# A graph attention layer: the mean row for nodes without edges in two float16 parts, and later waits in the first unit of a batch

## What is computed

```python
h = jnp.einsum('bnf,hfo->bhno', x, W)
s1 = jnp.einsum('bhno,ho->bhn', h, a1)
s2 = jnp.einsum('bhno,ho->bhn', h, a2)
e = leaky_relu(s1[..., :, None] + s2[..., None, :], negative_slope=0.2)
attn = softmax(where(adj > 0, e, -9e15), axis=-1)
h_prime = jnp.einsum('bhnm,bhmo->bhno', attn, h)
out = layernorm(x + h_prime.transpose(0, 2, 1, 3).reshape(B, N, H * Fo), axis=-1)
```

## Time and profile before

| what | value |
|---|---|
| time, median of 3 runs | 2936.99 us (2936.55 to 2944.32) |
| profiled execution, its time | 2935.6 us |
| its span, first to last instruction | 2933.7 us |
| PE busy | 2676.7 us (91%) |
| DVE busy | 2580.6 us (88%) |
| ACT busy | 2366.0 us (81%) |
| POOL busy | 823.3 us (28%) |

### The profile page before, as it was taken

One profiled execution on the slowest core, in us unless ns is written; L12 is line 12 of the kernel. 1 busy time (PEld: TensorE's weight loads), 2 busy tenths in 40 slices (PEclk: granted clock), 3 DMA queues, 4 the chain that ended last, 5 costly groups with the idle time before them and its releaser, 6 DMA issues.

```text
span 2933.7 us, 125924 instructions
## 1 busy us (share of the span) xinstructions
PE 2676.7 (91%) x52546; PEld 2318.7 (79%) x52546; DVE 2580.6 (88%) x3825; ACT 2366.0 (81%) x3950; POOL 823.3 (28%) x1011
## 2 busy tenths in 40 slices
PE   6999989989899898999989989899998999989996
PEld 3698867988579894898948988499884988859886
DVE  6899979998799997999889998899978999889896
ACT  4599964999559994699937998399983999839995
POOL 4522124221342214322152221521216222162221
PEclk9999999999999999999999999999999999999998
DMA  6567643676526754277533775347744477345763
GB/s 173 118 131 172 143 130 73 143 165 140 140 61 162 168 139 118 67 167 172 134 102 80 171 162 129 101 105 170 163 108 115 104 168 171 100 112 123 161 159 99
DMA packets 281205, 390.20 MB, mean 133 GB/s; under 512 B 161856, under 2 KB 161856, under 8 KB 280672
## 3 DMA queue, kind: packets, MB, share of 16 engines
q1 hardware_dynamic: 253536, 315.24, 41.6%
q0 software_dynamic: 27136, 67.12, 13.8%
HBM read 313.52 MB, written 34.14 MB: 119 GB/s over the span
## 4 chain that ended last, share of the span: by engine, by line
PE 31%; DVE 25%; ACT 22%; issue 16%; POOL 2%; DMA 2%; DVEq 1%; ACTq 0%; SPq 0%; POOLq 0%
ACT m_pos L602 20%; PE ps L525 11%; PE ps L556 6%; PE ps L557 6%; DVE m_neg L834 5%; PE ps L496 5%; DVE m_pos L827 3%; DVE m_pos L813 2%; DVE y L698 2%; DVE prod L800 2%; DMA y<-in_x 2%; ACT adj_cut L568 1%; DVE prod_d L803 1%; DVE total L665 1%; PE ps L432 1%
## 5 line engine op out<-in xcount | busy, mean ns | idle before, releaser
L602 ACT ACTIVATE m_pos<-ps,s_steep 128x512 fp8e4<-128x512 f32 x3496 | 2153.4, 1210 | 376.0 <-PE ps L446 281.9
L525 PE MATMUL ps<-b_both,m_pos 128*128 128x130 f16 x16384 | 1026.5, 222 | 113.1 <-DVE total L665 83.7
L525 PEld LDWEIGHTS ps<-b_both,m_pos 128*128 128x128 fp8e5 x16384 | 970.1, 99 | 127.5 <-issue 127.0
L557 PE MATMUL ps<-d_lo,m_neg 128*128 128x65 f16 x16384 | 1035.8, 194 | 24.1 <-issue 23.8
L556 PEld LDWEIGHTS ps<-d_hi,m_neg 128*128 128x128 fp8e5 x16384 | 1017.3, 98 | 37.4 <-issue 37.2
L556 PE MATMUL ps<-d_hi,m_neg 128*128 128x65 f16 x16384 | 1036.0, 193 | 4.0 <-issue 3.7
L557 PEld LDWEIGHTS ps<-d_lo,m_neg 128*128 128x128 fp8e5 x16384 | 1008.3, 98 | 19.4 <-issue 5.7
L827 DVE TENSOR_TENSOR m_pos<-m_pos,maskT 128x1024 uint32<-128x1024 uint32 x512 | 616.7, 1231 | 135.3 <-ACT m_pos L602 104.6
L834 DVE TENSOR_TENSOR m_neg<-m_pos,maskT 128x2048 uint32<-128x2048 uint32 x256 | 583.8, 2280 | 0.3
L496 PE MATMUL ps<-W_sb,xT 128*128 128x512 f32 x1024 | 459.4, 610 | 62.7 <-DVE prod_d L803 60.4
L568 ACT ACTIVATE adj_cut<-adj_in 128x1024 fp8e4<-128x1024 int32 x264 | 397.7, 1577 | 125.9 <-DMA adj_in<-in_adj 125.8
(11 more groups left out here) (95 smaller groups left out, 1606.7 us busy)
## 6 DMA issues: line engine op xcount, KB each, us to landing
adj_in<-in_adj SPq DMA_DIRECT2D x266, 512.0 KB, 4.9
s_bc<-s_rows SPq DMA_DIRECT2D x258, 256.0 KB, 3.8
x_in<-in_x SPq DMA_DIRECT2D x134, 256.0 KB, 4.7
x_sum<-in_x POOLq DMA_DIRECT2D x128, 256.0 KB, 5.8
y<-in_x POOLq DMA_DIRECT2D x32, 1024.0 KB, 9.8
out<-y SPq DMA_DIRECT2D x32, 1024.0 KB, 6.9
maskT<-adj_cut SPq DMA_TRANSPOSE x264, 4.0
m_neg<-in_x SPq DMA_DIRECT2D x10, 256.0 KB, 3.2
```

The source lines that it names most:

```text
L525: mm = pe.matmul(acc, mask, b_both[:, j, h, :, :], start=(j == 0 and it % 2 == 0), stop=(j == JC - 1 and it % 2 == 1))
L557: mm = pe.matmul(acc, mask, d_lo[:, j, h, :], start=False, stop=(j == JC - 1))
L602: ins = nc.scalar.activation(chunk(m_pos[h % 2], j, 0, BLK), ps[:, BANK_S1 + h % 2, :], ACT.Relu, bias=s2_steep[:, j, h:h + 1], scale=STEE ...
```

## The change

The mean row is cut into two float16 parts in place of three bfloat16 ones. `no_edge` multiplies the mean by the scale in partitions 0 to 63 (`mean_f`), casts it (`mean_part`), writes the cast to partition 0 of `mean_next` and the rest (float32 minus cast) to partition 32 (`LOW`). No memset and no multiplication with ident's columns is left. The very small constant moves from the mean row to the other operand, `tiny_bf`, in place of ones, and the product takes 64 partitions in place of 128. `mean_f` and `mean_next` are filled once at the start.

In PE's unit 0, quad 0 now waits for the low part b of chunk 7, quad 1 for that of chunk 12, and tile 0's j = 13, 14 and 15 each for their own. The wait for `hi_d_made` is gone, and x tile 0 is turned where the other tiles are: behind `spread_s1`, between the positive and the negative sums. Semaphores and tiles named tiny are named mean (those hunks are left out here). In PE's wait for the bank of the mean, `tiny_step` 6b + 1 is now `mean_step` 2b + 1.

```diff
@@ -86,6 +86,7 @@
+    LOW = 32
@@ -168,14 +169,15 @@
-        kappa_tiny = sb("kappa_tiny", [P, 1], F32)
+        kappa_mean = sb("kappa_mean", [P, 1], F32)
-        tiny_f = sb("tiny_f", [P, H, O1], F32)
-        tiny_part = sb("tiny_part", [P, H, O1], BF16)
-        tiny_next = sb("tiny_next", [P, H, O1], BF16)
-        tiny = sb("tiny", [P, H, O1], BF16)
+
+        mean_f = sb("mean_f", [P, H, O1], F32)
+        mean_part = sb("mean_part", [P, H, O1], F16)
+        mean_next = sb("mean_next", [P, H, O1], F16)
+        mean = sb("mean", [P, H, O1], F16)
@@ -487,7 +489,7 @@
-                        pe.wait_ge(tiny_step, 6 * b + 1)
+                        pe.wait_ge(mean_step, 2 * b + 1)
@@ -503,29 +505,31 @@
                         if unit == 0:
-                            pe.wait_ge(hi_d_made, b * JC + JC - 1)
-                            turn_x(JC * (b + 1), x_in[0][:], x_loaded[0], b * (JC // 2), 0)
-                            pe.wait_ge(tiny_made, b + 1)
-
-                            pe.wait_ge(lo_made, at(lo_made, 2 * JC * (b + 1) - 2))
+                            pe.wait_ge(mean_made, b + 1)
+
+                            pe.wait_ge(lo_made, at(lo_made, 2 * JC * b + JC - 1))
+                            pe.sem_inc(waited[pe.engine], 1)
                         pe.wait_ge(pos_read, at(pos_read, u))
                             pe.sem_inc(waited[pe.engine], 1)
+                            if unit == 0 and qd:
+                                pe.wait_ge(lo_made, at(lo_made, 2 * JC * (b + 1) - 7))
+                                pe.sem_inc(waited[pe.engine], 1)
                             for it in range(IT):
                                 for j in range(qd * JQ, (qd + 1) * JQ):
-                                    if unit == 0 and it == 0 and j == JC - 1:
-                                        pe.wait_ge(lo_made, at(lo_made, 2 * JC * (b + 1) - 1))
+                                    if unit == 0 and it == 0 and j >= JC - 3:
+                                        pe.wait_ge(lo_made, at(lo_made, 2 * JC * b + 2 * j + 1))
                                         pe.sem_inc(waited[pe.engine], 1)
                                     if j == 0:
-                                        pe.matmul(acc[:, 0:O1], ones_bf[:], tiny[:, h, :], start=False, stop=False)
+                                        pe.matmul(acc[:, 0:O1], tiny_bf[0:2 * LOW, :], mean[0:2 * LOW, h, :], start=False, stop=False)
                         mm.then_inc(pos_summed, 1)
@@ -535,7 +539,7 @@
                             turn_s1(b + 1)
-                        if unit and unit in TILE_UNIT:
+                        if unit in TILE_UNIT:
                             t = TILE_UNIT.index(unit)
@@ -739,30 +743,21 @@
                 dve.wait_ge(bound_step, 3 * n + 2)
                 V.tensor_scalar(kappa[:], bound_inv[:], SPLIT_TOP, None, ALU.mult)
-                V.tensor_scalar(kappa_tiny[:], bound_inv[:], SPLIT_TOP * TINY / N, None, ALU.mult
+                V.tensor_scalar(kappa_mean[:], bound_inv[:], SPLIT_TOP / N, None, ALU.mult
                                 ).then_inc(bound_step, 1)
                 dve.wait_ge(bound_step, 3 * n + 3)
-            def no_edge_start(n):
+            def no_edge(n):
+                both = slice(0, 2 * LOW)
                 dve.wait_ge(h_mean_summed, n + 1)
-                V.tensor_scalar(tiny_f[:, :, 0:O], ps[:, BANK_MEAN, :].rearrange("p (h o) -> p h o", h=H),
-                                kappa_tiny[:, 0:1], None, ALU.mult)
-                V.memset(tiny_f[:, :, O:O1], TINY * SPLIT_TOP).then_inc(tiny_step, 1)
-                dve.wait_ge(tiny_step, 6 * n + 1)
-
-            def no_edge_part(n, part):
-                V.tensor_copy(tiny_part[:], tiny_f[:]).then_inc(tiny_step, 1)
-                dve.wait_ge(tiny_step, 6 * n + 2 + 2 * part)
-                if part == 0:
-                    V.tensor_scalar(tiny_next[:], tiny_part[:], ident[:, 0:1], None, ALU.mult)
-                else:
-                    ins = V.scalar_tensor_tensor(out=tiny_next[:], in0=tiny_part[:], scalar=ident[:, part:part + 1],
-                                                 in1=tiny_next[:], op0=ALU.mult, op1=ALU.add)
-                if part < 2:
-                    V.tensor_tensor(tiny_f[:], tiny_f[:], tiny_part[:], ALU.subtract).then_inc(tiny_step, 1)
-                    dve.wait_ge(tiny_step, 6 * n + 3 + 2 * part)
-                else:
-                    ins.then_inc(tiny_next_made, 1)
+                V.tensor_scalar(mean_f[both, :, 0:O], ps[both, BANK_MEAN, :].rearrange("p (h o) -> p h o", h=H),
+                                kappa_mean[both, 0:1], None, ALU.mult).then_inc(mean_step, 1)
+                dve.wait_ge(mean_step, 2 * n + 1)
+                V.tensor_copy(mean_part[both], mean_f[both]).then_inc(mean_step, 1)
+                V.tensor_copy(mean_next[0:1], mean_f[0:1])
+                dve.wait_ge(mean_step, 2 * n + 2)
+                V.tensor_tensor(mean_next[LOW:LOW + 1], mean_f[LOW:LOW + 1], mean_part[LOW:LOW + 1], ALU.subtract
+                                ).then_inc(mean_next_made, 1)
             def turn_s2(n):
@@ -778,8 +773,8 @@
                 V.tensor_scalar(d_hi[:, :, :, O], e_d[:], SPLIT_TOP, None, ALU.mult).then_inc(den_hi_made, 1)
-                dve.wait_ge(tiny_next_made, b + 1)
-                V.tensor_copy(tiny[:], tiny_next[:]).then_inc(tiny_made, 1)
+                dve.wait_ge(mean_next_made, b + 1)
+                V.tensor_copy(mean[:], mean_next[:]).then_inc(mean_made, 1)
                 dve.wait_ge(den_hi_made, b + 1)
@@ -849,7 +844,7 @@
-            V.memset(ones_bf[:], 1.0).then_inc(ones_bf_made, 1)
+            V.memset(tiny_bf[:], TINY).then_inc(tiny_bf_made, 1)
@@ -858,7 +853,8 @@
-            V.memset(tiny_f[:], TINY * SPLIT_TOP).then_inc(setup_step, 1)
+            V.memset(mean_f[:], SPLIT_TOP)
+            V.memset(mean_next[:], 0.0).then_inc(setup_step, 1)
@@ -940,10 +934,7 @@
                         if unit == STAT_UNIT + 2:
-                            no_edge_start(b + 1)
-                            no_edge_part(b + 1, 0)
-                            no_edge_part(b + 1, 1)
-                            no_edge_part(b + 1, 2)
+                            no_edge(b + 1)
                         take_neg(u, h, k * IT)
```

More of the change, by code:

```diff
@@ L189, in gat_kernel @@
         ones = sb("ones", [P, P], F32)
-        ones_bf = sb("ones_bf", [P, P], BF16)
+        tiny_bf = sb("tiny_bf", [P, P], BF16)
         w_loaded = sem("w_loaded")
@@ L201, in gat_kernel @@
         consts_made = sem("consts_made")
-        ones_bf_made = sem("ones_bf_made")
+        tiny_bf_made = sem("tiny_bf_made")
         ident_made = sem("ident_made")
@@ L237, in gat_kernel @@
         h_mean_summed = sem("h_mean_summed")
-        tiny_step = sem("tiny_step")
-        tiny_next_made = sem("tiny_next_made")
-        tiny_made = sem("tiny_made")
+        mean_step = sem("mean_step")
+        mean_next_made = sem("mean_next_made")
+        mean_made = sem("mean_made")
         r_row_made = sem("r_row_made")
@@ L466, in _ @@
             pe.wait_ge(consts_made, 1)
-            pe.wait_ge(ones_bf_made, 1)
+            pe.wait_ge(tiny_bf_made, 1)
             for i in range(JC):
@@ L891, in _ @@
             exponents(0)
-            no_edge_start(0)
-            for part in range(3):
-                no_edge_part(0, part)
+            no_edge(0)
             with nc.Fori(0, B, engines=[dve.engine], hint_back_edge=True) as b:
```

## The result

The changed kernel takes 3001.7 us (median of 4 runs, 2994.35 to 3005.73) against 2937.89 us before (4 runs, 2936.55 to 2944.32): a ratio of 1.0198, 95% interval 1.0183 to 1.0213 (the quotient of the two medians is 1.0217). It is 2% slower, where 2925.2 us and "faster" were forecast. The profiled execution took 2994.35 us.

The account below looks back on a forecast made before the run. Bound: DVE and ACT waiting in turn at seven batch ends, then PE from unit 0's last low part, later ACT. Sum: 2935.6 − 21.2 − 2.3 − 1.5 + 3.4 + 11.2 = 2925.2 us; range 2912 to 2935.

Parts of the forecast that it names:

- The step that failed: PE's mean product over 64 partitions: taken to cost nothing extra, from the spread row's product with 96.
- The bound of 0.8 us a unit: Upper bound for the 64-partition products: a whole product's 195 ns each instead of being hidden in PE's stream.
- The sign that the prediction itself named for being wrong: In PE's profile after: a unit's positive sums taking longer around the small products; no size given.
- broken stream: Rival: 64-partition products break PE's stream, 0.1 to 0.195 us each, 51 to 100 us, 2976 to 3025 us; chance 0.06.
- The mean row: DVE's cut at batch ends: 2.25 us instead of 5.28, 3.0 saved; `take_pos` of unit 30 to `batch_start` 20.9 us.
- the three terms of the mean row: DVE's shorter cut: −21.2 us at seven batch ends, −2.3 at the program's start, −1.5 at the very end.
- The term for the very end: After the last batch, DVE's last read of negative sums: at most 1.5 of the 3.0 us arrive, −1.5.
- The earlier start of unit 0: PE's unit 0 starts about 471.9 instead of 474.39, worth nothing: POOL's last low part still holds tile 0's j = 15.
- The turn and the clock: PE's unit 0: moved turn of x tile 0, +3.4 us; half clock behind a 3.2 us hole, +11.2.
- paid in full: Work added to PE behind the last low part in unit 0 reaches the end at full length.

Follow-up runs that it names:

- the last kernel above: The new mean row with its product over 128 partitions and the whole first unit as before, in the kernel before: 2911.73 us, ratio 0.9916.
- the grouped products: The changed kernel with a unit's four 64-partition products one behind another at the end of quad 0: 2950.32 us, ratio 1.0035.
- half and for all of the changes: The kernel before with the mean product over 64 partitions for two of a unit's four row tiles (2978.61 us) or for all four (3019.72 us).

## Why the prediction was wrong

**The step that failed** is in the part on the mean row: "For a product with fewer than 128 partitions the nearest row is the spread with 96 ... I take nothing." The row was read rightly, and it is true for 96. It was taken for all heights under 128. 1024 products, each between two of 128 partitions, cost 0.21 us each in place of nothing: 214 us more work for TensorE, of which the end pays 80 (3001.7 − 2921.85). The bound of 0.8 us a unit that stood beside it was nearly the true value, 0.84. The sign that the prediction itself named for being wrong, positive sums that take longer around the small products, is what the trace shows. The rival "broken stream" had the place, nearly the price (0.1 to 0.195 a product, measured 0.21) and the time (2976 to 3025), and got 0.06. That the time fell inside its range is in part luck: it had the full price paid for half of the products, and the end paid 37% of a price just above its highest. With a bound of a whole product on 1024 uses, and no row of the height in question, it deserved far more, and the range should have reached to it.

The Trainium skill ("TensorE: Matmul & The Clock Gate", section "LDWEIGHTS (loading the stationary operand)") says that a load's time goes with its columns, and that 32 rows take as long as 128. The traces agree for the load itself (91 to 99 ns at every height); what changes is when it starts (104.8 us of idle time ahead of 1024 loads, against 0.0).

**The mean row** was right: 2.26 us against 2.25, seven ends at 20.9 to 21.0 against 20.9. With the full product, old first unit or new with the turn ahead, the kernel gains 0.79% to 0.87% in four measurements, 23 to 26 us; the three terms of the mean row come to 25 (21.2 + 2.3 + 1.5). The profiles place it: from `take_pos` of unit 30 to `batch_start` the seven ends take 167.5 us before and 146.7 in the last kernel above, 20.8 less, and the first `batch_start` comes 2.8 us earlier. The term for the very end is unsure: from the last such `take_pos` it is 33.0 us before and 31.3 to 33.4 with the new mean row.

**The earlier start of unit 0** was forecast at nothing and is nothing that can be told: equal times with old and new waits (2911.73 and 2912.20).

**The turn and the clock** had the right sign and too large a size: 14.6 forecast, 10.4 and 6.5 measured. The hole is there (3.26 against 3.2), the clock falls in seven of seven and not four of five, for 4.2 us of work against 4.0. Right behind the hole the half clock costs 1.5 us a batch, 10.3 in seven, against 11.2 forecast. So the local terms were not much too large; less of them arrives at the end than the forecast's "paid in full", and where the rest goes is open. In the changed kernel itself the slow units leave a hole of only 2.4 us, with half clock behind four of seven.

**The sum.** With the failed term at nothing the forecast was 2925.2; the kernel in which that term is nothing, with 128 partitions, measured 2921.85.

## What to carry to other kernels

Fewer partitions in a matmul were not free where it stood between full ones: with 64 or 32 of them, each change of height cost TensorE about 0.10 us here, three times the small product's own step of 0.03. If the spare rows can hold zeros, take all 128; if not, put the low products together. Watch the idle time of the weight loads, not the products' durations: those stayed within 4% here. And before a wait that sets a stage's end, do not gather PE's work in one piece if other work can stand in the hole: with the turn moved out of it one hole of 3.3 us was left, the clock fell behind it every time, and turn and clock together cost the end 5 to 10 us. Products without use in the hole kept the clock up, and no gain at the end could be measured.

## What the runs showed that I had not expected

A product 96 high follows one 128 high nearly without loss (0.06 and 0.03 us, as a full one), and one 64 high costs as much as one 32 high (4.59 and 4.58 us a unit). Four products 64 high follow each other every 0.04 us. And of TensorE's added work the end paid the same share, 38%, for half and for all of the changes (41 of 107 us, 81 of 214), though 53% for the grouped products. Much of the rest went into waits: PE's time without work was 257.0 us before and 154.0 with all products 64 high (3017.8 − 2863.8).
